# Moving normalisation and token marks to GpSimd, counting experts with additions, and taking the first batch's row maxima by query halves

## The reference, cut to what matters

```
x: 4 batches x 1024 tokens x 256 channels, float32 (4096 tokens, 32 tiles of 128)
x = x + 0.5 * ffn0(layernorm(x))            # int-quantised gate/up/down, hidden 704
x = x + attn0(layernorm(x))                 # 16 heads of 16, rotary, no mask
x = x + 0.5 * ffn0(layernorm(x))
x = x + 0.5 * mixture(layernorm(x))         # as below
x = x + attn1(layernorm(x))                 # 16 heads of 16, ALiBi, causal
x = x + 0.5 * mixture(layernorm(x))

attn:    softmax(q k^T / 4 [+ bias + mask]) v, then an output projection
mixture: inp -> x = w_norm * rms(inp); probs = softmax(x @ w_router)   # 32 experts
         w, sel = top_k(probs, 4)
         each expert takes the tokens that chose it, in token order, at most 128
         out = sum w * expert(x) + sigmoid(x @ w_shared_gate) * shared_ffn(x)
         return inp + out
```

## Time and profile before

| | |
|---|---|
| time, median of 3 runs (lowest, highest) | 2843.71 us (2838.93, 2847.15) |
| time of the profiled execution | 2837.38 us |
| its span, first to last instruction | 2835.6 us |
| mean granted TensorE clock | 0.960 |
| busy: PE, DVE, ACT, POOL | 2615.9, 1945.1, 1269.8, 655.7 us |

### The profile page before, as it was taken

The page is one execution under the profiler, slowest core; times in us unless marked ns, Lnnn a source line. Parts: engine busy times, 40 slices in busy tenths (PEclk is TensorE's granted clock), DMA queues, the critical chain, the costliest instruction groups (busy, mean ns, idle before and its releaser), DMA issues. The chain is left out here.

```text
span 2835.6 us, 38818 instructions
## 1 busy us (share of the span) xinstructions
PE 2615.9 (92%) x14164; PEld 1255.9 (44%) x14164; DVE 1945.1 (69%) x4168; ACT 1269.8 (45%) x1936; POOL 655.7 (23%) x640
## 2 busy tenths in 40 slices
PE   5888999999999999787898997999999999898998
PEld 3442333333333332344555654454445554555665
DVE  6968878778787885685774335777667675576334
ACT  3431566566566667443212322355455556321221
POOL 1544223232141200253002440212121110001441
PEclk9996999999999999998999999799999999999999
DMA  3003330321303400002202654633134330301565
GB/s 122 1 17 89 51 62 18 57 47 28 57 24 51 62 1 2 1 1 80 80 34 67 153 118 121 98 69 61 42 53 68 63 57 2 112 34 34 126 161 157
DMA packets 162593, 175.78 MB, mean 62 GB/s; under 512 B 19090, under 2 KB 135762, under 8 KB 162258
## 3 DMA queue, kind: packets, MB, share of 16 engines
q1 hardware_dynamic: 146948, 152.57, 24.8%
q0 software_dynamic: 12416, 17.84, 3.8%
q10 hardware_dynamic: 3040, 2.88, 0.4%
HBM read 116.32 MB, written 56.13 MB: 61 GB/s over the span
## 5 line engine op out<-in xcount | busy, mean ns | idle before, releaser
L1820 DVE TENSOR_REDUCE a_mx<-a_bank 128x1 f32<-128x512 f32 (+3 forms) x1792 | 1036.6, 627 | 263.2 <-PE a_bank L1554 183.1
L1690 ACT ACTIVATE a_E<-a_bank 128x1024 f32<-128x1024 f32 (+3 forms) x896 | 796.1, 931 | 459.4 <-PE a_bank L1611 313.4
L1554 PE MATMUL a_bank<-a_KT,a_QT 96*128 96x512 bf16 (+4 forms) x1792 | 593.7, 376 | 25.3 <-DVE a_mx L1820 16.2
L1611 PE MATMUL a_bank<-a_QT,a_KT 99*128 99x512 bf16 (+4 forms) x1792 | 509.1, 359 | 4.2 <-DMA a_QT<-a_mT 2.3
L1626 PE MATMUL a_bank<-a_E,a_Vg 128*32 128x512 f32 (+3 forms) x3584 | 437.7, 560 | 0.7 <-ACT a_E L1690 0.7
L1554 PEld LDWEIGHTS a_bank<-a_KT,a_QT 96*128 96x128 bf16 (+1 forms) x1792 | 151.9, 98 | 514.4 <-DVE a_mx L1820 323.5
L1611 PEld LDWEIGHTS a_bank<-a_QT,a_KT 99*128 99x128 bf16 (+1 forms) x1792 | 170.7, 99 | 175.9 <-ACT a_E L1690 30.9
L983 ACT ACTIVATE d_silu<-d_bank 128x512 f32<-128x512 f32 x96 | 57.2, 596 | 367.6 <-PE d_bank L857 367.6
L872 PE MATMUL d_bank<-wdT,d_hT 128*128 128x256 f32 (+1 forms) x768 | 198.4, 402 | 4.2 <-DVE d_hT L1072 4.2
L433 POOL TENSOR_TENSOR f_hl<-f_hT,f_hh 128x512 f16<-128x512 f32 x96 | 111.9, 1166 | 353.2 <-ACT f_hh L450 351.3
L776 POOL DMA_INDIRECT d_xg<-normalised,d_index x64 | 67.5, 1054 | 518.2 <-issue 516.7
(11 more groups left out here) (239 smaller groups left out, 3521.8 us busy)
## 6 DMA issues: line engine op xcount, KB each, us to landing
parts<-a_parts SPq DMA_DIRECT2D x64, 384.0 KB, 2.6
a_QT<-parts SPq DMA_DIRECT2D x180, 128.0 KB, 5.8
a_KT<-parts SPq DMA_DIRECT2D x180, 128.0 KB, 9.0
d_wgu<-in_L_ffn_w_gate SPq DMA_DIRECT2D x64, 176.0 KB
d_wgu<-in_L_ffn_w_up SPq DMA_DIRECT2D x64, 176.0 KB
d_wd<-in_L_ffn_w_down SPq DMA_DIRECT2D x64, 176.0 KB
normalised<-d_xn SPq DMA_DIRECT2D x8, 1152.0 KB, 4.7
acc<-d_zero SPq DMA_DIRECT2D x2, 4224.0 KB, 15.5
```

What stands on the lines that cost most here:

```text
L1554: last = nc.tensor.matmul(out[:, 0:w], QT[0:W, h, qt * P:(qt + 1) * P], KT[0:W, h, kh * HALF:kh * HALF + w], start=True, stop=not diag)
L1611: last = nc.tensor.matmul(out, KT[:, h, kt * P:(kt + 1) * P], QT[:, h, half * HALF + c0:(half + 1) * HALF], start=True, stop=not diag)
L1690: nc.scalar.activation(E[:, u % 2, 2 * pair:2 * pair + 2, c0:HALF], bank[:, 2 * pair:2 * pair + 2, c0:HALF], ACT.Exp).then_inc(exps, 1)
L1820: nc.vector.tensor_reduce(mx[:, x[1] // C % 2, j, qt, kh:kh + 1], out[:, 0:w], AX.X, ALU.max).then_inc(freed_dve, 1)
```

## The change

In `ffn0_phase` the last mean step and the four `normalise` of the chunks from the third on go from VectorE to GpSimd: two in slot 4 and two in slot 5, ahead of the `hl` of these slots. `statistics` and `aggregate` on VectorE are spread anew over the slots.

In `mixture_phase` all but the first eight `normalise` go to GpSimd, and so do the products that make `marks`: one of 1024 elements and eight of 128 for each step. `choose` is cut in two (`highest` in slot 2, `choose` in slot 3), `count_experts` goes to slot 4 and `rank` to slot 5. The count is now two additions over pairs in place of a reduction, a cast and eight linked additions; the eight running sums become one carried sum, and TensorE adds the earlier tiles itself: one product with `tri` over 256 columns, one with the carried sum over 256, and seven shifted ones over 224 down to 32 columns.

In `attention_phase` the maxima of the first four groups are taken for each half of the queries, so there are 20 sets of rows (`row_sets`) instead of 16. The opening ends after 52 chunks in the first attention and after 48 in the second. The loop catches up by 9 chunks in two units (4, 5, 4, 5 ...) over its first 56 or 40 units. From there on it issues what it did. Units wait for the rows of their own half.

```diff
@@ ffn0_phase, gpsimd
+                def normalise(c, i):
+                    t = c * CT + i
+                    if i == 0:
+                        pool.wait_ge(meaned, START + c * 3 + 2)
+                        nc.gpsimd.tensor_scalar(mean[:], mean[:], 1.0 / D, None, ALU.mult).then_inc(meaned, 1)
+                        pool.wait_ge(turned, START + c * CT)
+                        pool.wait_ge(meaned, START + (c + 1) * 3)
+                    nc.gpsimd.tensor_scalar(xn[:, i, :], core.x[:, t, :], mean[:, i:i + 1],
+                                            core.rstd[:, t:t + 1], ALU.subtract, ALU.mult).then_inc(normed, 1)
...
+                        if j >= 4 and c + 2 < NCH:
+                            for i in (2 * j - 8, 2 * j - 7):
+                                normalise(c + 2, i)
@@ ffn0_phase, vector
+                        if more and 1 <= j <= 2:
+                            mean_step(c + 2, j - 1)
+                        if j == 0 and c > 1:
+                            statistics((c - 1) * CT - 1)
+                            for t in range((c - 2) * CT, (c - 1) * CT):
+                                aggregate(t)
+                        if j >= 3 and c:
+                            statistics((c - 1) * CT + j - 3)
@@ mixture_phase, gpsimd
+                def mark(r):
+                    pool.wait_ge(masked, START + r + 1)
+                    if r:
+                        pool.wait_ge(tabled, START + r * RT)
+                    nc.gpsimd.tensor_scalar(marks[:, 1], hot[:], core.const("token_lo")[:, 0:1], None, ALU.mult)
+                    for i in range(RT):
+                        t = r * RT + i
+                        last = nc.gpsimd.tensor_scalar(marks[:, 0, i], hot[:, i], core.const("token_hi")[:, t:t + 1], None, ALU.mult)
+                    last.then_inc(marked, 1)
...
+                for i in range(RT):
+                    normalise(1, i)
+                for r in range(NS):
+                    if r + 2 < NS:
+                        for i in range(RT // 2):
+                            normalise(r + 2, i)
+                    mark(r)
+                    if r + 2 < NS:
+                        for i in range(RT // 2, RT):
+                            normalise(r + 2, i)
@@ mixture_phase, tensor
-                    for i in range(RT):
-                        nc.tensor.matmul(ranks[:, i, :], tri[:], mask[:, i, :], start=True, stop=False)
-                        last = nc.tensor.matmul(ranks[:, i, :], ones[:], before_[:, i, :], start=False, stop=True)
+                    nc.tensor.matmul(ranks, tri[:], mask[:], start=True, stop=False)
+                    if r:
+                        nc.tensor.matmul(ranks, ones[:], spread(before_[:, r % 2, :], 1, RT), start=False, stop=False)
+                    for d in range(1, RT):
+                        last = nc.tensor.matmul(ranks[:, d:RT, :], ones[:], mask[:, 0:RT - d, :], start=False, stop=d == RT - 1)
...
-                    if j == 4 and c < NS:
+                    if j == 5 and c < NS:
                         rank(c)
@@ mixture_phase, vector
-                    link(r, nc.vector.tensor_reduce(count[:], hot[:].rearrange("p i k e -> p i e k"), AX.X, ALU.add))
-                    nc.vector.tensor_copy(mask[:], count[:])
-                    link(r, nc.vector.tensor_copy(before_[:, 0, :], before_[:, RT, :]))
-                    for i in range(RT):
-                        last = nc.vector.tensor_tensor(before_[:, i + 1, :], before_[:, i, :], mask[:, i, :], ALU.add)
...
+                    link(r, nc.vector.tensor_tensor(pairs[:], hot[:, :, 0:2, :], hot[:, :, 2:4, :], ALU.add))
+                    nc.vector.tensor_tensor(mask[:], pairs[:, :, 0, :], pairs[:, :, 1, :], ALU.add).then_inc(masked, 1)
@@ attention_phase
+    U0 = sum(1 for h, _, _ in units if h == 0)
+    C0 = C * U0 // U if second else C // 2
+    FIRST = C0 + (32 if second else 20)
+    def issued(n):
+        return min(FIRST + 9 * n // 2, C + AHEAD + C * n // U)
+    row_sets = [(G, h) for G in range(BG) for h in ((0, 1) if G < NG else (None,))]
...
-    opening = ahead_of_rows + some(0, C + 3) + [("turn_m", 0)] + some(C + 3, C + AHEAD)
+    opening = ahead_of_rows + some(0, C0 + 3) + [("turn_m", 0)] + some(C0 + 3, FIRST)
...
-    beside = {(n // U, n % U): some(C + AHEAD + C * n // U, C + AHEAD + C * (n + 1) // U) for n in range(BG * U)}
+    beside = {(n // U, n % U): some(issued(n), issued(n + 1)) for n in range(BG * U)}
@@ attention_phase, sync: rows(0) goes ahead of the last two writes of the first batch
-                for n in range(4, NJ):
-                    write(0, n)
+                write(0, 4)
+                write(0, 5)
                 rows(0)
+                write(0, 6)
+                write(0, 7)
@@ attention_phase, tensor
-                    pe.wait_ge(m_rows, START + (G + 1) * GH * 16)
                     for u in range(U):
+                        if (G, u) in at_unit:
+                            pe.wait_ge(m_rows, START + (at_unit[G, u] + 1) * GH * 16)
```

More of the change, by code:

```diff
@@ L839, in enter @@
                     for k in range(TOPK):
-                        last = nc.tensor.matmul(bank[:, 7, 0:VALS * NE], spots[:, i, k, :], marks[:, i, k].rearrange("p v e -> p (v e)"),
+                        last = nc.tensor.matmul(bank[:, 7, 0:VALS * NE], spots[:, i, k, :], marks[:, :, i, k, :],
                                                 start=(r == 0 and i == 0 and k == 0), stop=(r == NS - 1 and i == RT - 1 and k == TOPK - 1))
@@ L1137, in locate @@
                     nc.vector.tensor_tensor(hotr[:], hot[:], spread(ranks, 2, TOPK), ALU.mult).then_inc(ranks_used, 1)
-                    if r:
-                        dve.wait_ge(tabled, START + r * RT)
-                    own = spread(vals[:, r * RT:(r + 1) * RT, :], 3, NE)
-                    for k in range(TOPK):
-                        last = nc.vector.tensor_tensor(marks[:, :, k], spread(hot[:, :, k, :], 2, VALS), own, ALU.mult)
-                    last.then_inc(marked, 1)
                     dve.wait_ge(ranks_used, START + r + 1)
@@ L1220, in _ @@
                         if j == 2:
+                            highest(c)
+                        if j == 3:
                             choose(c)
-                        if j == 3:
+                        if j == 4:
                             count_experts(c)
-                            assert done == STEPS, done
+                            if c < NS - 1:
+                                carry(c)
                         if j == 5:
                             locate(c)
-                    if c < NS - 1 and 1 <= j <= 4:
-                        for i in range(2):
-                            normalise(c + 1, 2 * (j - 1) + i)
                     if 0 < c < NS and j in (0, 1):
@@ L1284, in attention_phase, with complete @@
     AHEAD = (5 if second else 4) * C // U
-    m_unit = next(u for u in range(U) if AHEAD + C * u // U >= C)
+    U0 = sum(1 for h, _, _ in units if h == 0)
[4 more added lines that the diff above has]
+    row_sets = [(G, h) for G in range(BG) for h in ((0, 1) if G < NG else (None,))]
+    at_unit = {(G, u): row_sets.index((G, h)) for G, h in row_sets for u in (U0 if h else 0,)}
+    def complete(k):
+        G, h = row_sets[k]
+        return G * C + (C0 if h == 0 else C)
+    m_unit = [next(n for n in range(BG * U) if issued(n) >= complete(k)) if k else -1 for k in range(len(row_sets))]
+    for k, (G, h) in enumerate(row_sets):
+        assert k == 0 or m_unit[k] + 3 < G * U + (U0 if h else 0), (k, m_unit[k])
+    measured = {m_unit[k]: k for k in range(1, len(row_sets))}
     y_unit = 2 + next(u for u in range(U) if units[u][0])
@@ L1320, in attention_phase @@
         beside[G, y_unit].insert(0, ("turn_y", G, 0))
-        if G + 1 < BG:
-            beside[G, m_unit + 2].insert(0, ("turn_m", G + 1))
-        else:
+        for u in range(U):
+            if G * U + u - 2 in measured:
+                beside[G, u].insert(0, ("turn_m", measured[G * U + u - 2]))
+        if G + 1 == BG:
             for u, kind, k in ((1, "turn_o", 0), (2, "turn_o", 1), (3, "out", 0), (4, "out", 1)):
@@ L1461, in _ @@
                 load(0, 1)
[L1462 to L1463 removed]
+                write(0, 4)
+                write(0, 5)
                 rows(0)
+                write(0, 6)
+                write(0, 7)
                 load(0, 2)
                 load(0, 3)
[L1467 removed]
+                todo = [(m_unit[k] + 2, rows, (k,)) for k in range(1, len(row_sets))]
                 for b in range(1, B):
@@ L1897, in _ @@
                     for u in range(U):
-                        step = 0 if u == m_unit and G + 1 < BG else 5
-                        if step == 0:
-                            maxima(G + 1, 0)
+                        k = measured.get(G * U + u)
+                        step = 0 if k else 5
+                        if k:
+                            maxima(k, 0)
```

145 lines of the change are left out of this document (74 added, 71 removed).

## The result

The changed kernel took 2855.51 us, median of 8 runs (2850.37 to 2865.23), beside 2844.69 for the kernel before (8 runs, 2838.93 to 2848.86). The ratio is 1.005, with a 95% interval of 1.0037 to 1.0063: slower by half a per cent, where 46 us less were forecast. So the two traces differ by 25 us, the medians by 11.

What follows compares the result with a forecast made beforehand. TensorE was taken to bound the attention loops, VectorE the openings, and late VectorE work the FFN and routing phases. Terms -8 - 4 - 11 - 23 = -46 us gave a median of 2798 us, range 2779 to 2822.

Steps and rivals of the forecast that it cites:

- T: FFN phases: the price of one normalisation on GpSimd, taken as 0.55 us between bounds from a copy and two-input instructions.
- The sum that led from T to the waits: FFN phases: 1.75 us of TensorE waits a chunk, 11.3 us a phase instead of 17.1; about -11 us for both.
- T between 0.75 and 1.0: Rival, FFN phases: GpSimd is the slow one; at T = 1.0 they give +10, 2819 us; chance 0.12.
- over 1.5: Rival, FFN phases: a GpSimd normalisation takes over 1.5 us; at 2 us +58, 2867 us; chance 0.04.
- -16.8: First attention: the opening loses 28 chunks of 0.60 us each, so it is 16.8 us shorter.
- +8.8 for the loop: First attention: the loop pays 6.1 us for the 28 chunks, 2.4 for backlog and 0.3 for four transposes.
- 2.4 for backlog: First attention's loop: VectorE's backlog reaches TensorE in units of five chunks; 2.4 us taken between nothing and 5.
- The rival of a bound by VectorE: Rival: VectorE becomes the bound of the attention loops, the 12 us of both attentions vanish, 2810 us; chance 0.12.
- 9.8: Second attention: of 11.0 us from the 49th chunk to the first score 1.2 stay, so the opening gives 9.8.
- -23 forecast: Both mixtures: -12.3 us in d4 and -10.6 in d6, from xn, ranks, spots and the clock.
- Term (1): Mixtures: GpSimd has the xn tiles ready long before, so TensorE's 2.7 us wait for xn goes.
- The rival of a blocked interface: Rival, d4 and d6: GpSimd beside VectorE's two-input instructions loses 12 us on the path, 2810 us; chance 0.07.

Runs made afterwards that it cites:

- ffn_only: The kernel before with the two FFN phases changed alone: 2870.99 us, ratio 1.0096.
- ffn_half: The kernel before with the FFN phases changed alone, each GpSimd normalisation over 128 of 256 channels (timing only): 2837.38 us, ratio 0.9982.
- a2_heavy: The kernel before with the first attention changed alone, its 28 caught-up chunks placed by units and projection and value product amid their unit's chunks: 2830.68 us, ratio 0.9953.
- mix_only: The kernel before with the two mixtures changed alone: 2809.91 us, ratio 0.9887.
- mix_marks: The kernel before with the mixtures changed, and the eight short GpSimd products of marks replaced by one two-input product of 1024 elements: 2808.61 us, ratio 0.9887.
- ffn_spread: The kernel before with changed FFN phases alone, one GpSimd normalisation in each of slots 2 to 5, mean steps moved up: 2829.92 us, ratio 0.9944.

## Why the prediction was wrong, step by step

**The FFN phases: T was mis-sized, by a bound taken from another kind of instruction.** "I take the middle, T = 0.55", between a copy and a two-input instruction. It measured 1.22, and the two phases cost 27 us (ffn_only) where 11 were to be gained. The sum that led from T to the waits was right in its slope and some 4 us too high in its level: it gives 17.1 us of waits in a phase at T = 0.79 and 6 x 4.43 + 0.8 = 27.4 at 1.22, while f1 had 12.9 in ffn_half (7.2 for `hT`, 4.0 for `hl`, 1.7 for `xn`) and 23.0 in the changed kernel (7.2, 3.6, 12.2), the last chunk's 4.5 left out. So the waits of f1 grew by 5.9 us, and the phase by 16. Most of the rest is the low clock, which the forecast counted for d4 and forgot here: 0.92 on the mean over the 183 us of f1 against 0.96 over 167 before, by estimate 183 x 0.08 - 167 x 0.04 = 8 us. That the sum with the true T, +10 for a phase, comes as near to +16 as it does is luck: 4 us too much for waits stand against 8 left out for the clock. The rivals left a hole: "T between 0.75 and 1.0" and "over 1.5", with the truth between them. The place of the wait was a little off too: I had it at `down_proj`, but `turn` stands ahead of it and reads the tiles themselves. The Trainium skill (GPSIMD Engine Reference, "Performance versus the Vector engine") has 1.03 cycles for an element of a body of up to two operations, which at 1.2 GHz would be 0.22 us for these 256 by estimate, the start not counted. The trace doesn't agree: from 128 to 256 elements the instruction grew from 0.79 to 1.22 us, 3.3 ns for an element, four times as much, and the measurement decides.

**First attention: the gain was right, the price in the loop was half of what it is.** -16.8 came to the microsecond in the trace of the whole change (15.4 to 16.8 in four traces). Of the +8.8 for the loop, the term "2.4 for backlog" failed: the loop lost 16.6 to 18.5. VectorE was busy for 85% of the stretch, less than the 92% that I had worked out, and it still ran behind. Waits shown are 7.1 us against 1.6. After each of the 23 waits a product also stands alone instead of overlapping its neighbour, 0.38 us in place of 0.22, some 3.7 us by estimate. Together that is about 9 us where I had 2.4; the rest of the loss no run splits. The rival of a bound by VectorE had it, with a chance of 0.12. That it is VectorE's backlog and not a fixed price of a chunk, a2_heavy shows: the same chunks and the same VectorE work at other places cost 6.4 us less.

**Second attention: three terms.** From the last product of d4 to the first score the opening gave 9.4 us of 9.8 (8.5 to 9.6 in the other traces). The wait for rows was 3.8 and 6.4 where I took 1: I had looked at what stands behind `rows` on the queue, not at the 24 loads ahead of it, which kept the DMA engines busy; and from the issue to the unit that needs the rows were 3.95 us, where I had two units of 3. The rest is the backlog, as in the first.

**The mixtures: mechanism right, size too small in mix_only.** -23 forecast, -23.4 in the traces of the whole change, -32 (-27 to -37) by the ratio of mix_only. So the close agreement with the traces of the whole change is partly luck. Term (1) was the small one: 2.7 us for `xn` in each, where 15 us in both hang on those instructions. The rival of a blocked interface fell: a `spots` took 0.71 us beside GpSimd, 0.69 without. The Trainium skill (SBUF — State Buffer, "Who interferes with whom") has as a rule that a VectorE instruction with two SBUF inputs contends with a GpSimd one that reads SBUF. The traces agree, but here it was mostly GpSimd that paid: its short products took 1.31 to 1.53 us beside `spots`, 0.60 otherwise, and 0.60 beside VectorE's instructions that read PSUM. In mix_marks it was VectorE, up to 2.38 us, and the time stayed the same.

**Chances.** 0.93 for faster was too much for a sum in which two prices, T and the loop with five chunks in a unit, had no row.

## What to carry to other kernels

When work moves to an engine on which no row shows that instruction, rows of other instructions bound nothing: here it took 2.2 times the middle of such bounds. Ask what the change gives at two or three times your price. Ask where it stands before how long it is: the same four normalisations cost 27 us in a burst ahead of a consumer and gained 16 us one to a slot. And where two engines are nearly balanced, extra work belongs into the units in which the other engine is busy with something else.

## What the runs showed of the hardware

- GpSimd's `tensor_scalar` on 128x256 float32 takes 0.85 us with one constant, 1.21 to 1.22 with two operations and two scalars of the partition, 0.79 in that form on 128x128; `tensor_tensor` on 128x256 takes 0.72. VectorE takes 0.41 for the same normalisation while GpSimd is idle. In bf16 with 1024 elements `tensor_scalar` takes 2.84 against 1.95 for `tensor_tensor`, with 128 elements still 0.60.
- GpSimd and VectorE held each other up where VectorE read two tiles of SBUF: a GpSimd product of 0.60 us took 1.31 to 1.53 beside `spots`, and `spots` stayed at 0.69 to 0.71 on the mean. Beside GpSimd's two-input product of 1.95 us one `spots` in each mixture took 2.38.
- Four small DMAs took 10.4 us from the first issue to the product that reads them with 24 loads of 128 KB issued ahead of them and a DMA share of 1.08 over 20 us, 6.5 us in the kernel before, where the share was 0.01 over the 5 us of their issue.
- The granted clock was 0.93 on the mean over 120 us of f1 with 20.7 us of waits, and 1.00 with 15.0 us of them in the kernel before and 9.2 in ffn_spread. In the mixtures 17.9 us less of routing waits came with 32 us less time.
